# Distances of batches 2 and 3 as two one-pass products, and new step orders, in a four-batch LoRA, cross-attention and graph kernel

## The reference, cut to what matters

```
# L0: routed LoRA
w    = softmax(x @ router_W.T + router_b)                    # 8 experts
upd  = sum_n w[:, n] * (a_sum @ lora_B[n].T)                 # rank 64
x1   = nan_to_num(x + 0.5 * upd)
# L1: cross-attention, 32 heads of 16, then residual and layer norm
Q, K, V = x1 @ Wq.T + bq, ctx @ Wk.T + bk, ctx @ Wv.T + bv
attn = softmax(Q K^T / 4 where mask else -inf)
points = layernorm(x1 + (attn V) @ Wo.T + bo) * ln_g + ln_b
# L2 and L3: two graph layers of four blocks, on the same neighbour lists
d2  = |y_n|^2 + |y_m|^2 - 2 <y_n, y_m>                       # y = columns of ctx: 512 nodes, 64 long
idx = top_k(-d2, 8)                                          # 8 nearest of each node
for each of 2 x 4 blocks:
    p = leaky_relu(points)
    points = (W_block p + sum over the 8 neighbours of W_block p) / 9 + points
```

## Time and profile before

| | |
|---|---|
| runs | 377.03, 377.60, 379.24 us; median 377.60 |
| profiled execution, span | 378.0 us, 6569 instructions (no other time of it is given) |
| busy of the span | PE 367.6, DVE 272.0, ACT 177.0, POOL 129.0 us |
| TensorE clock granted, mean | 0.995 of full speed |

### The profile page before, as it was taken

One profiled execution on the slowest core, in us unless ns is written; L12 is line 12 of the kernel. 1 busy time (PEld: TensorE's weight loads), 2 busy tenths in 40 slices (PEclk: granted clock), 3 DMA queues, 4 the chain that ended last, 5 costly groups with the idle time before them and its releaser, 6 DMA issues.

```text
span 378.0 us, 6569 instructions
## 1 busy us (share of the span) xinstructions
PE 367.6 (97%) x2396; PEld 311.0 (82%) x2396; DVE 272.0 (72%) x427; ACT 177.0 (47%) x308; POOL 129.0 (34%) x125
## 2 busy tenths in 40 slices
...
GB/s 201 317 348 159 24 55 155 78 9 178 34 20 232 105 0 116 102 0 3 0 3 2 0 0 2 0 2 1 2 0 2 0 2 0 3 0 2 0 85 139
DMA packets 25056, 22.47 MB, mean 59 GB/s; under 512 B 9537, under 2 KB 20546, under 8 KB 25026
## 3 DMA queue, kind: packets, MB, share of 16 engines
...
q10 hardware_dynamic: 674, 0.02, 0.1%
...
## 4 chain that ended last, share of the span: by engine, by line
PE 85%; DVE 4%; ACT 4%; DMA 3%; issue 2%; SPq 1%; DVEq 0%; ACTq 0%
PE slot L564 82%; DMA wk<-in_WkT 3%; ACT k_blk_hi L943 2%; PE slot L684 1%; PE slot L693 1%; SPq L448 1%; PE slot L725 1%; ACT probT L976 1%; DVE p_full L1321 1%; DVE points L1331 1%; ACT adj L874 1%; DVE inv_full L1267 0%; ACT L976 0%; DVE stats L1282 0%; DVE shift L1255 0%
## 5 line engine op out<-in xcount | busy, mean ns | idle before, releaser
L1065 POOL TENSOR_TENSOR p_lo<-p_full,p_hi 128x512 fp32r<-128x512 f32 x64 | 86.0, 1362 | 157.1 <-ACT p_hi L1016 157.0
L1026 ACT ACTIVATE u_hi<-slot 128x512 fp32r<-128x512 f32 x64 | 36.2, 593 | 69.3 <-PE slot L564 69.0
L1326 DVE TENSOR_TENSOR u_lo<-slot,u_hi 128x512 fp32r<-128x512 f32 x64 | 42.4, 684 | 31.5 <-ACT u_hi L1026 31.5
L1016 ACT ACTIVATE p_hi<-p_full 128x512 fp32r<-128x512 f32 x64 | 39.0, 627 | 55.3 <-DVE p_full L1321 55.3
L564 PE MATMUL slot<-adj,u_hi 128*128 128x512 f32 x256 | 64.8, 392 | 0.1
L564 PE MATMUL slot<-fs_hi,p_hi 128*128 128x256 f32 x256 | 64.8, 286 | 0.0
L1331 DVE SCALAR_TENSOR_TENSOR points<-slot,points 128x512 f32<-128x512 f32 x64 | 42.7, 684 | 30.4 <-PE slot L564 30.4
L564 PE MATMUL slot<-adj,u_lo 128*128 128x512 f32 x256 | 64.1, 391 | 0.0
L564 PE MATMUL slot<-fs_lo,p_hi 128*128 128x256 f32 x256 | 64.1, 283 | 0.0
L1321 DVE SCALAR_TENSOR_TENSOR p_full<-points 128x512 f32<-128x512 f32 x64 | 54.3, 863 | 8.9 <-POOL p_lo L1065 6.3
L564 PEld LDWEIGHTS slot<-adj,u_lo 128*128 128x128 f32 x256 | 47.5, 188 | 10.1 <-issue 0.4
...
## 6 DMA issues: line engine op xcount, KB each, us to landing
q_stack<-q_hi SPq DMA_DIRECT2D x32, 128.0 KB, 2.5
...
q_stack<-q_lo SPq DMA_DIRECT2D x16, 128.0 KB, 2.4
...
```

The lines of the kernel that those rows point to most:

```text
L1016: act.activation(p_hi[b][:, (i % 2) * H:(i % 2 + 1) * H], p_full[:, p_buf[b, i]], ACT.Copy)\
L1026: act.activation(half_of(u_hi[:, u], i % 2), bank("wa", b, i // 2, i % 2), ACT.Copy)\
L1065: pool.tensor_tensor(lo[:, cut], full[:, cut], hi[:, cut].bitcast(F32), ALU.subtract)\
L1326: dve.tensor_tensor(half_of(u_lo[:, u], i % 2), bank("wa", b, i // 2, i % 2), half_of(u_hi[:, u], i % 2).bitcast(F32), ALU.subtract).then_ ...
```

## The change

For batches 2 and 3 the distances are no longer float32 products. The 128 contracted rows carry two things at once, a high and a low half, and two `fp32r` products are summed in PSUM: `row_hi2` by `col_hi_lo`, and `row_lo` by `col_hi_sq`. The four operands lie in `k_stack`, which the last attention has to release first (step `sq2` waits for the last `w3`). What prepares them is new: six DMAs a batch instead of two, `sq` with three ACT instructions instead of one, a POOL step `sp` with five, an ACT step `sr` with three, and one DVE memset `sm`. Batches 0 and 1 keep theirs. All five orders are new, and the PSUM banks with them.

```
 def load_xyz(b):
+    if b < 2: ...                       # as before: 2 DMAs
+    for rows in (0, V):                 # b >= 2: 6 DMAs
+        load(xyz[b][rows:rows + V, :], ctx[b], f"xyz{b}")
+        load(xyz_n[b][rows:rows + V // 2, :], ctx[b, V // 2:V], f"xyz{b}")
+        load(xyz_n[b][rows + V // 2:rows + V, :], ctx[b, 0:V // 2], f"xyz{b}")
 # tensor engine
+elif kind == "dist" and b >= 2:
+    after(pe, stack_ready, "sr", b)
+    pe.wait_ge(halves_set, 1)
+    cut = slice(i * P, (i + 1) * P)
+    mm(bank("dist", b, i), row_hi2[:, cut], col_hi_lo, True, False)
+    mm(bank("dist", b, i), row_lo[:, cut], col_hi_sq, False, True).then_inc(dist_done, 1)
 # scalar engine
+if kind == "sq" and b >= 2:
+    loaded(act, f"xyz{b}", 6)
+    after(act, weights_done, "w", B - 1, KC - 1)   # b == 2; for b == 3: dist2_3 done
+    act.activation(row_hi2, xyz[b], ACT.Copy).then_inc(row_hi_ready, 1)
+    act.activation(sq_sum[:], xyz[b], ACT.Square)
+    act.activation(xyz_n[b], xyz_n[b], ACT.Square).then_inc(sq_ready, 1)
+elif kind == "sr":
+    after(act, stack_lo, "sp", b, each=2)
+    x_rows = xyz[b][0:V, :]
+    act.activation(col_hi_lo[0:V], x_rows, ACT.Copy)
+    act.activation(col_hi_sq[0:V], x_rows, ACT.Copy)
+    act.activation(col_hi_sq[V + V // 2:P], sq_lo[V + V // 2:P], ACT.Copy).then_inc(stack_ready, 1)
 # gpsimd
+elif kind == "sp":
+    pool.wait_ge(row_hi_ready, b - 1)
+    after(pool, sq_ready, "sq", b)
+    link(pool.tensor_tensor(sq_sum[:], sq_sum[:], xyz_n[b], ALU.add))
+    link(pool.tensor_copy(col_hi_sq, sq_sum[:]))
+    pool.tensor_tensor(sq_lo[:], sq_sum[:], col_hi_sq.bitcast(F32), ALU.subtract).then_inc(stack_lo, 1)
+    pool.tensor_tensor(row_lo[0:V], xyz[b][0:V, :], row_hi2[0:V].bitcast(F32), ALU.subtract)
+    pool.tensor_tensor(col_hi_lo, xyz[b], row_hi2.bitcast(F32), ALU.subtract).then_inc(stack_lo, 1)
 # vector engine
+elif kind == "sm":
+    dve.memset(row_lo[V:P].bitcast(F32), -0.5).then_inc(halves_set, 1)
```

More of the change, by code:

```diff
@@ L47 @@
 PE_STEPS = """
[L48 to L62, removed]
@@ L73 @@
-gc3_7 gd3_7 ga1_7:3,7 gb1_7 gc1_7 gd1_7
+mb0:0 dist0_0:4 dist0_1:2 dist0_2:6 dist0_3:5 lora0:7 router0:1 keys:2,3 mixed0:5,0 adjT0:6,7 ua0:5,1 ub0 uc0
+lora1:2 dist1_0:5 dist1_1:6 router1:4 qa0:7,0 dist1_2:2 qb0 qc0 mixed1:3,1 lora2:4 ua1:2,3 sc0_1:0,1 sc0_2:4,5
+router2:6 ub1 sc0_0:0,1 uc1 sc0_3:4,5 values:0,1 dist1_3:2 mixed2:4,5 shift0:3 qa1:7,6 qb1 qc1 ua2:1,0 ub2 w0_0:4,5
+sc1_1:6,7 uc2 w0_1:2,3 lora3:6 w0_2:4,5 at0_0:0,1,2 at0_1 w0_3:6,7 router3:3 sc1_2:4,5 at0_2 at0_3 qa2:7,6 sc1_0:0,1
+norm0:4,5 qb2 qc2 sc1_3:4,5 rows0:0,1 oa0 shift1:5 mixed3:2,3 ob0 oc0 sc2_0:2,3 sc2_1:4,5 ua3:6,7 sc2_2:0,1 ub3
@@ new lines @@
+w1_0:4,5 w1_1:2,3 w1_2:0,1 uc3 at1_0:4,5,6 at1_1 w1_3:2,3 adjT1:0,1 at1_2 at1_3 sc2_3:2,3 qa3:1,0 shift2:2 qb3 qc3
+wa0_0:3,7,1 wb0_0 wc0_0 norm1:4,5 wd0_0 ga0_0:6,2 gb0_0 sc3_1:4,5 gc0_0 gd0_0 w2_0:4,5 rows1:6,7 sc3_0:0,1 sc3_2:2,3
+sc3_3:4,5 oa1 w2_1:2,3 w2_2:0,1 ob1 at2_0:2,3,4 oc1 shift3:5 w2_3:0,1 at2_1 at2_2 wa0_1:6,7,0 wb0_1 wc0_1 at2_3
+wd0_1 ga0_1:1,0 wa1_0:6,5,1 wb1_0 gb0_1 norm2:2,3 gc0_1 wc1_0 wd1_0 gd0_1 ga1_0:7,2 gb1_0 w3_0:4,5 gc1_0 w3_1:0,1
+gd1_0 w3_2:6,7 at3_0:0,1,3 at3_1 w3_3:4,5 wa1_1:6,7,1 wb1_1 at3_2 at3_3 wc1_1 rows2:5,4 oa2 wd1_1 ob2 oc2 norm3:6,7
```

121 lines of the change are left out of this document (70 added, 51 removed).

## The result

The changed kernel takes 385.81 us (384.83 to 388.08), the kernel before 377.4 us (377.03 to 379.24) in four runs each: a ratio of 1.0225 (95% interval 1.0187 to 1.0264). The forecast was 374.1 us in a range to 377.2, so even the sign was wrong. The profiled spans show the same loss: 378.0 before, 386.2 after. A run's time is its own span and some 1.8 us. The profiled execution of after, too, is the longest of its four (388.08 us).

What follows compares the result with a forecast made beforehand. PE's work was taken as the bound, plus its few stops and a fixed start and tail. 378.0 - 3.3 of work - 0.2 of stops = 374.5 us; the median 0.4 lower, 374.1, range 371.0 to 377.2.

Steps and rivals of the forecast that it cites:

- The work removed: PE's eight distances of batches 2 and 3: two 0.23 us products replace each 0.88 us float32 one, saving 3.3 us.
- The fifth rival: The two new products per distance run as float32 ones do, 0.88 us each: 384.8 us, chance 0.02.
- The new waits: PE's waits on new chains: `dist2` covered by 2.8 us, `dist3` by 5, a stop of 1.0 at `w3_0`.
- The fourth rival: At `dist2_0` the stack's chain is late, POOL's five instructions taking 11 us: 379.5 us, chance 0.08.
- the second rival: Attention windows too short, SP's 16.3 us binding at `w2_0` and `w3_0`: 6.5 us of stops, 376.6 us, chance 0.13.
- new stops ... 4.0 us: PE's stops after the change: 1.0 + 0.3 + 1.5 and 1.2 of small ones, 4.0 us against 4.2 before.
- Early front: At PE's start `ua0`, `qa0` and `qb3` wait for late inputs: 1 to 2 us of stops together.
- my third rival: Ten new POOL instructions each hold DVE up to 1.1 us, 2 us reaching PE: 376.1 us, chance 0.07.
- a fall in the middle: Sign of being wrong: the granted clock falls anywhere in the middle, since every sum is made at full clock.

Runs made afterwards that it cites:

- e9: The changed kernel with the edits of e4, e5 and e6, `rc0` ahead of `xl2_1` on DVE and `uh0_2` ahead of `ph1_0` on ACT: 376.70 us.
- e10: The orders of e9 with float32 distances for batches 2 and 3, without `sp`, `sr` and `sm`: 379.13 us.
- e4: The changed kernel with POOL's `zb` and `zk` ahead of `lbl` and ACT's `wqh` ahead of `mh0_0`: 382.30 us.
- e1: The kernel before with all five new orders alone, distances left in float32, without `sp`, `sr` and `sm`: 387.49 us.
- e3: The changed kernel with one swap in SP's list, `qs0` ahead of `sd0`: 388.71 us.
- e5: The changed kernel with `wv` under the second `adj` buffer instead of `q_stack`, without SP's wait on `values`: 383.82 us.
- e6: The changed kernel with three moves in DVE's list: `al2_1` before `rc3`, `pt0_4` before `lk2_1`, `ul1_6` before `pt3_0`: 383.61 us.
- e7: The changed kernel with the edits of e4, e5 and e6, `rc0` ahead of `xl2_1` on DVE and `dev1` behind `ex2_3` on ACT: 379.40 us.

## Why the prediction was wrong

**The work removed: right.** The group of all sixteen new products of after:

```profile
L577 PE MATMUL slot<-k_stack 128*128 128x512 f32 x16 | 4.9, 398 | 0.0
```

The two of `dist2_0` start at 184.17 and their successor at 184.63, 0.46 us as the forecast had it, where a float32 one took 0.88. (The 398 ns are records that overlap.) The fifth rival is refuted. Of the 3.3 us e9 against e10 shows 2.4 in the time and 3.0 in PE's busy time (367.6 to 364.6).

**The new waits: right, as far as they are waits of data.** `sp2` took 6.0 us and `sp3` 6.3, against 6.0 forecast. `sr2` was done at 179.4 and `dist2_0` ran at 184.2, covered by 4.8 (forecast 2.8), though the memset `sm`, which `dist2_0` needs too, ended only at 182.6: DVE has it late in its list, and the forecast gave it no wait; `sr3` at 205.5 and `dist3_1` at 210.9, covered by 5.4 (forecast 5). `oa3` and `wb2_0` didn't wait. `w3_0` stopped 0.37 us (forecast 1.0; it is 1.02 in e9). The fourth rival, and the second at the place that it named, are refuted. The table loads came to five in the stretch, as forecast.

**The step that failed: "new stops ... 4.0 us".** They were 14.3. Three terms were missing or too small. Slower had a chance of 0.09, and nearly all of that for a late chain of `sp2` and `sr2`, which isn't what happened.

1. *Early front, "1 to 2 us".* It was 3.85: `ua0`, `router1`, `qa0`, `qb0`. I had walked the data that `ua0` and `qa0` need, and put `ml0_0` 0.4 us late, but not laid POOL's list beside DVE's. There `wql` and `zk` stood right over `nan0_0`; e4 shows this by removal. Two further stops, `qa2` 1.47 and `norm0` 0.88, come where POOL's `zr` and `wol` (77.9 to 89.8 us) run beside `nan2_1`, which takes 4.5 us, and `xl2_0`. After above, e4 below:

```profile
83.27 6.55 POOL L1101 TENSOR_TENSOR wo_lo<-wo_raw,adj 128x512 fp32r<-128x512 f32 x4
86.94 1.74 DVE L1293 TENSOR_TENSOR x_lo<-x,x_hi 128x512 fp32r<-128x512 f32 x1
...
80.76 5.52 POOL L1101 TENSOR_TENSOR wo_lo<-wo_raw,adj 128x512 fp32r<-128x512 f32 x4
79.77 0.77 DVE L1293 TENSOR_TENSOR x_lo<-x,x_hi 128x512 fp32r<-128x512 f32 x1
```

   In after, e1 and e3 `wol` starts about 3.7 us ahead of `xl2_0`, which takes 1.7 us, and `qa2` stops by 1.5 to 1.8. In e4, e5, e6, e7, e9 and e10 it starts 1.0 us behind, `xl2_0` takes 0.8, and `qa2` doesn't stop. No run moved `wol` by itself, but the nine traces agree, e6's too, whose lists are those of after up to there. For `norm0` the cause is read from the overlap alone; 0.66 us is left there in e9.
2. *`w0_0`, not in the sum at all.* I walked SP's chain for `w1_0`, `w2_0` and `w3_0`. For `w0_0` I didn't ask what the first stack waits for besides its data: the room that `wv` held. `values` moved back by 27 us and became what SP waits for: its start came 4.5 us later than before, and the stop is 2.44 us. e5 shows it. After that stop comes a stretch at half clock, of after:

```profile
77.00:80.00 3.00, 3.00 (x16) 3.00 (x16) 1.73 (x2) 0.57 (x1) 2.42 (x6) 0.50 0.00 0
```

   It costs 1.7 us. The profiled execution of before has a like one at 17.2 us, behind a wait of 2.4 us for `wk`, so in the difference of the two spans it counts as moved. In the medians it doesn't. Of before's 43 executions beside the experiments 11 have a mean clock of 0.995 and take 378.7 to 379.8 us; the others take 376.8 to 377.6. Of after's four, three have 0.996 (385.61 to 388.08) and one 1.000 (384.83). So of the 8.4 us between the medians perhaps 1 is the clock, an estimate from that one run. The forecast had named a fall in the middle as a sign of being wrong.
3. *POOL holds DVE, my third rival, at 2 us and a chance of 0.07.* By the new `sp` alone it is 2.4 us (`ob2` 1.54, `ga1_2` 0.82; both absent in e1), so that size was near. The chance was the mistake, and that I tied the mechanism to the ten new instructions: the same cause, through POOL steps that were only moved, makes 3.4 us at `router1` to `qb0` and 0.95 at `gc1_3` (a `p_full` of 1.80 us beside a `p_lo`; e6 removes the stop by taking that `p_full` out of its way). In all 6.7 us by those six places, and 9.1 with `qa2` and `norm0`. This is the largest part of the loss. The rule of the Trainium skill that I cited ("SBUF — State Buffer", "Who interferes with whom"), two SBUF inputs against a GpSimd instruction that reads SBUF, is borne out in this: e4, with POOL elsewhere, has the SCALAR_TENSOR_TENSOR of `nan0_0` at 0.69 us, where after has 1.64.

**What it adds up to.** The three repairs alone give 3.5, 2.0 and 2.2 us, 7.7 together, of the 8.4 by which after's median lies above before's. The sum is no proof that these are all, since each trace also lacks `qa2`'s stop; what is shown is that all together, with `rc0` and `uh0_2` moved, take 9.1 us off (385.81 to 376.70). The mended orders with float32 distances (e10) are still 1.7 us slower than before; the products' 2.4 us turn that into a gain of 0.8. Where e10's 1.7 us lie was not followed up; its trace still has stops of 0.81 us at `at2_3`, 0.78 at `w3_0` and 0.70 at `norm0`, as e9's has (0.81, 1.02 and 0.66).

**Slips in the rivals' sums.** None of them carries the forecast. The terms of the second rival give 4.4 us of stops, 5.6 with the small ones, and not 6.5. In the fourth, a `sp` of 11 us passes the two covers of `oa3` and `wb2_0` by 0.2 and 2.3 us rather than 0.5 and 2.7. The fifth comes to 384.6.
